# Output products for two pairs at a time, an output bias added by POOL, and a new order of slots in a gated attention and expert kernel

## What is computed

```python
def _L0_xattn_ref(Q, K, V, Wq, Wk, Wv, Wo):          # 16 heads, DK = DV = 64
    scores = einsum('bhqd,bhkd->bhqk', q, k) / sqrt(DK), causal mask
    out = einsum('bhqk,bhkd->bhqd', softmax(scores), v)
    return out.reshape(b, sq, H * DV) @ Wo

def _L0_ffn_ref(x, ...):
    h = _rmsnorm(x, gamma1)
    q = h @ Wq + bq;  k, v = split((h @ Wdown + bdown) @ Wup + bup)
    att = softmax(einsum('bthd,btgd->bthg', q, k) / sqrt(8))   # over the 16 heads of a row
    x = x + (einsum('bthg,btgd->bthd', att, v).reshape(b, t, D) @ Wo + bo)
    h2 = _rmsnorm(x, gamma2)
    gate = softmax(h2 @ Wg + bg)
    return x + einsum('btd,edf,bte->btf', h2, We, gate)

x = x + tanh(g_xattn[0]) * _L0_xattn_ref(_layernorm(x), ctx, ctx, Wq, Wk, Wv, Wo)
x = x + tanh(g_ffn[0]) * _L0_ffn_ref(_layernorm(x), ...)
```

## Time and profile before

| what | value |
|---|---|
| median of 3 runs | 261.29 us (259.64 to 261.53) |
| time of the profiled run | 261.93 us |
| its span | 259.9 us |
| PE busy | 245.6 us, 94% |
| DVE busy | 192.4 us, 74% |
| ACT busy | 171.6 us, 66% |
| POOL busy | 149.9 us, 58% |

### The profile page before, as it was taken

One profiled execution on the slowest core, in us unless ns is written; L12 is line 12 of the kernel. 1 busy time (PEld: TensorE's weight loads), 2 busy tenths in 40 slices (PEclk: granted clock), 3 DMA queues, 4 the chain that ended last, 5 costly groups with the idle time before them and its releaser, 6 DMA issues.

```text
span 259.9 us, 7887 instructions
## 1 busy us (share of the span) xinstructions
PE 245.6 (94%) x3244; PEld 178.7 (69%) x3244; DVE 192.4 (74%) x333; ACT 171.6 (66%) x501; POOL 149.9 (58%) x157
## 2 busy tenths in 40 slices
PE   7989989998899999999999999988999897979995
PEld 4765877785867677676859595858676462858774
DVE  0237644189998989898998842799989999786964
ACT  2437634756687787978787778566877676472454
POOL 4104041264646686969696835778466995867320
PEclk9999999999999999999999999999999998899999
DMA  6990000000000000000000000000000000000000
GB/s 208 359 320 21 3 4 3 3 1 3 3 3 0 3 10 3 15 0 15 1 3 13 3 11 3 13 3 10 3 0 5 11 14 3 11 0 3 10 13 20
DMA packets 6017, 7.30 MB, mean 28 GB/s; under 512 B 477, under 2 KB 4830, under 8 KB 5982
## 3 DMA queue, kind: packets, MB, share of 16 engines
q1 hardware_dynamic: 5550, 6.16, 7.5%
q10 hardware_dynamic: 432, 0.64, 0.7%
HBM read 5.88 MB, written 0.92 MB: 26 GB/s over the span
## 4 chain that ended last, share of the span: by engine, by line
PE 70%; DVE 18%; ACT 5%; issue 4%; POOL 1%; DVEq 0%; POOLq 0%
PE ps_a L875 40%; PE ps_c L875 9%; PE ps_b L875 8%; PE ps_e L875 7%; PE ps_b L927 4%; DVE ps_e L665 3%; DVE prod L683 3%; DVE ps_e L694 2%; ACT probs L446 2%; DVE nmax L626 2%; PE ps_b L872 1%; DVE psums L631 1%; DVE fqkv L649 1%; POOL prod L326 1%; PE ps_c L971 1%
## 5 line engine op out<-in xcount | busy, mean ns | idle before, releaser
L326 POOL TENSOR_TENSOR prod<-fqkv 128x1280 f32<-128x1280 f32 (+1 forms) x14 | 38.7, 2761 | 10.3 <-DVE fqkv L649 10.3
L316 POOL TENSOR_TENSOR probs<-probs,prinv 120x672 f32<-120x672 f32 x16 | 24.3, 1518 | 31.1 <-DVE prinv L635 31.1
L334 POOL TENSOR_TENSOR prod<-e_sb,fqkv 128x768 f32<-128x768 f32 (+1 forms) x14 | 24.5, 1753 | 21.3 <-ACT e_sb L474 21.3
L875 PEld LDWEIGHTS ps_a<-aT,wo_sb 128*128 128x128 f32 x256 | 30.8, 196 | 4.4 <-ACT v_sb L435 2.6
L875 PE MATMUL ps_a<-aT,wo_sb 128*128 128x112 f32 x256 | 32.1, 279 | 0.4 <-ACT aT L440 0.3
L875 PE MATMUL ps_a<-wv_sb,cT 128*64 128x512 f32 x128 | 32.3, 620 | 0.0
L665 DVE TENSOR_REDUCE ps_e<-prod 128x256 f32<-128x2048 f32 x13 | 29.7, 2287 | 0.0
L694 DVE TENSOR_REDUCE ps_e<-prod 128x128 f32<-128x2048 f32 x13 | 29.7, 2285 | 0.0
L875 PE MATMUL ps_a<-cT,wk_sb 128*128 128x224 f32 x128 | 28.6, 375 | 0.0
L429 ACT COPY kT<-ps_a 128x448 f32<-128x448 f32 x32 | 17.1, 533 | 16.2 <-PE ps_a L875 16.2
L875 PE MATMUL ps_a<-xT,wqc 128*128 128x224 f32 x128 | 27.1, 361 | 0.6 <-ACT qT L429 0.6
(11 more groups left out here) (144 smaller groups left out, 487.9 us busy)
## 6 DMA issues: line engine op xcount, KB each, us to landing
xp_sb<-in_xp SPq DMA_DIRECT2D x1, 896.0 KB, 7.9
out<-out_sb SPq DMA_DIRECT2D x14, 64.0 KB, 1.5
xT<-in_x_t SPq DMA_DIRECT2D x1, 784.0 KB, 9.5
cT<-in_ctx_t SPq DMA_DIRECT2D x1, 784.0 KB, 11.1
wv_sb<-in_wv SPq DMA_DIRECT2D x1, 512.0 KB, 8.1
wo_sb<-in_wo SPq DMA_DIRECT2D x1, 512.0 KB, 12.7
fwe_sb<-in_fwe SPq DMA_DIRECT2D x1, 512.0 KB, 8.8
fw_sb<-in_fw SPq DMA_DIRECT2D x1, 266.0 KB, 13.1
```

The lines of the kernel that those rows point to most:

```text
L316: nc.gpsimd.tensor_tensor(pr[0:TG, NC:C, :, 0:S], pr[0:TG, NC:C, :, 0:S], prinv[p % 2][0:TG, NC:C, :].unsqueeze(3).to_broadcast([TG, C - N ...
L326: nc.gpsimd.tensor_tensor(o, k, q, ALU.mult).then_inc(s["prod1_pool"], 1)
L334: nc.gpsimd.tensor_tensor(o, e, v, ALU.mult).then_inc(s["prod2_pool"], 1)
L875: return nc.tensor.matmul(o, lhsT, rhs, start=start, stop=stop, skip_group_check=True)
```

## The change

The first eight pairs are done two at a time in `new_y` and `new_x1`: one output product of 8 matmuls with 224 columns instead of two with 112 (`Y_UNITS`), in slots 2, 4, 6 and 8. Pair 0's product is no longer in the start. Since a tile may need both pairs of a unit, the slot that starts no tile is now slot 3, not slot 9 (`tile_steps`). `aT` is one tensor of two halves. `bias_o` is gone from PE; ACT scales `xc` in place (`scaled_x`), POOL adds the bias row (`biased`), and DVE's `new_x2` is a plain addition. The two warm-up products are seven of 128 columns. The order within the slots changes on all four engines.

```diff
+DOUBLE = 8
+Y_UNITS = [(p, p + 1) for p in range(0, DOUBLE, 2)] + [(p,) for p in range(DOUBLE, NP)]
+Y_AT = {unit[-1] + 1: n for n, unit in enumerate(Y_UNITS)}
+def units_for(f):
+    return next(n + 1 for n, unit in enumerate(Y_UNITS) if (unit[-1] + 1) * T >= (f + 1) * 128)
+def tile_steps():
+    steps, last = {}, 0
+    for f in range(NT):
+        last = max(last + 1, Y_UNITS[units_for(f) - 1][-1] + 1)
+        steps[last] = f
+    return steps
...
-        aT = two("aT", [128, C, T])
+        aT = sb("aT", [128, C, 2 * T])
...
+            def biased(f):
+                pool.wait_ge(s["u_ready"], f + 1)
...
+                nc.gpsimd.tensor_tensor(xc[f % XB][:, :], xc[f % XB][:, :], fw_sb[:, COL_BO:COL_BO + D], ALU.add).then_inc(s["ub_ready"], 1)
...
+            def scaled_x(f):
+                act.wait_ge(s["centred"], f + 1)
+                act.wait_ge(s["rstd2_ready"], f + 1)
+                nc.scalar.activation(xc[f % XB][:, :], xc[f % XB][:, :], ACT.Copy, scale=rstd2[f % XB][:, 0:1]).then_inc(s["u_ready"], 1)
...
-                nc.vector.scalar_tensor_tensor(out=x2[f % 2][:, 0:D], in0=xc[f % XB][:, :], scalar=rstd2[f % XB][:, 0:1], in1=ps_c[:, 1, 0:D],
-                                               op0=ALU.mult, op1=ALU.add).then_inc(s["x2_ready"], 1)
+                dve.wait_ge(s["ub_ready"], f + 1)
+                nc.vector.tensor_tensor(x2[f % 2][:, 0:D], ps_c[:, 1, 0:D], xc[f % XB][:, :], ALU.add).then_inc(s["x2_ready"], 1)
...
-            for n in (4, 3):
-                nc.tensor.matmul(ps_b[:, 0, 0:n * 128], ident[:, :], ident[:, :].unsqueeze(1).to_broadcast([128, n, 128]), start=True, stop=True)
+            for _ in range(7):
+                nc.tensor.matmul(ps_b[:, 0, 0:128], ident[:, :], ident[:, :], start=True, stop=True)
...
-                    ins = mm(ps_a[:, 0, 0:T], wo_sb[:, ch, :], aT[p % 2][:, ch, :], start=(ch == 0), stop=(ch == C - 1))
+                    ins = mm(ps_a[:, 0, 0:w], wo_sb[:, ch, :], aT[:, ch, c0:c0 + w], start=(ch == 0), stop=(ch == C - 1))
...
-                mm(ps_c[:, 1, 0:D], ident[:, :], fw_sb[:, COL_BO:COL_BO + D], stop=False)
```

More of the change, by code:

```diff
@@ L48, in sums_made @@
     return sum((by_pe.get(n, 0) > 0) + (by_pe.get(n, 0) < FH) for n in range(f + 1))
[L51 to L57, removed]
+DOUBLE = 8
[9 more added lines that the diff above has]
+    return steps
+TILE_AT = tile_steps()
+LAST_STEP = max(TILE_AT) + 2
 TAIL = 14
@@ L410, in _ @@
             second_scale(prior)
+            biased(last)
             gating(prior)
@@ L439, in attended @@
                 act.wait_ge(a_full[b], n)
-                nc.scalar.copy(aT[p % 2][:, 4 * half:4 * half + 4, :],
+                nc.scalar.copy(aT[:, 4 * half:4 * half + 4, p % 2 * T:(p % 2 + 1) * T],
                                ps_a[:, b, 0:4 * T].rearrange("p (c t) -> p c t", c=4)).then_inc(a_free[b], 1)
@@ L545, in _ @@
                     squares(fc)
+                if t < NP:
+                    exps(t)
+                if fc is not None:
                     x2_copy(fc)
@@ L550, in _ @@
                     head_exps(fb)
+                    scaled_x(fb)
+                if fc is not None:
+                    gate_exps(fc)
                 if t < NP:
@@ L603, in _ @@
             x2_copy(last)
+            experts(prior, 1)
             experts(prior, 0)
-            experts(prior, 1)
             gate_exps(last)
@@ L798, in _ @@
                     new_x2(fc)
+                if fb is not None:
+                    logits(fb)
+                if t in Y_AT:
+                    new_x1(Y_AT[t])
                 if t < NP:
                     prob_sums(t)
-                if t <= NP:
-                    new_x1(t - 1)
-                if t < NP:
                     norm(t)
                 if fb is not None:
-                    logits(fb)
                     shifted_logits(fb)
@@ L850, in _ @@
             shifted_logits(last)
+            gate_sum(third)
             head_scales(prior)
-            gate_sum(third)
             normed_heads(prior)
             weighted(last)
+            head_scales(last)
             new_x2(prior)
-            head_scales(last)
             head_sums(last)
@@ L859, in _ @@
             gate_logits(prior)
+            new_x2(last)
             gate_sum(prior)
-            new_x2(last)
             gate_logits(last)
@@ L1159, in _ @@
             turn_o(prior)
-            bias_o(prior)
             new_o(prior)
```

151 lines of the change are left out of this document (78 added, 73 removed).

## The result

The changed kernel takes 263.08 us (median of 11 executions, 262.4 to 264.8), the kernel before 260.95 (11, 259.5 to 261.8): a ratio of 1.0126, interval 1.0097 to 1.0155. The forecast was 258.1, faster. The profiled execution took 262.78 us with a span of 261.0.

The account below looks back on a forecast made before the run. PE was taken to set the pace, DVE 1.3 us behind in a full slot. Gains of 1.5 + 2.3 + 0.75, 4.5 us, less 1.3 for a lowered clock, gave 258.7, against the median 258.1 us; range 255.6 to 261.8.

Follow-up runs that it names:

- b_bias: The kernel before with only the output bias moved from PE (ACT scales the centred rows, POOL adds the bias), all orders kept: 262.16 us, 1.0078.
- b_warm: The kernel before with only its two warm-up products (512 and 384 columns) replaced by seven of 128 columns: 262.52 us, 1.0098.
- b_pad40: The kernel before with ten tiny products (40 more PE instructions) in PE's idle time ahead of the first scores: 262.71 us, 1.0085.
- a_pad36: The changed kernel with nine tiny products (36 more PE instructions) added: 267.65 us, 1.0276 against the kernel before.
- a_sums35: The changed kernel with DVE's probability sums and norm ahead of its logits in slots 3 and 5 only: 264.91 us, 1.0186 against the kernel before.
- b_pad112: The kernel before with 28 tiny products (112 more PE instructions) ahead of the first scores: 270.41 us, 1.0407.
- a_oldwarm: The changed kernel with the old two warm-up products (512 and 384 columns), 20 fewer records: 262.41 us, 1.0072 against the kernel before.

## What to carry over

Before taking a product's length off a busy engine, look at what the next instruction there waits for: two starts and the end of the copy between them show whether the product was cover. A product moved to another engine can delay a third: in b_bias POOL's bias addition moved its products onto DVE's scaling. Compare profiles with the granted clock of many executions in hand, since the one profiled may be unusual by more than the change. And where a loss appears in rows that the change didn't touch, count PE's instructions up to it: an edit of 20 instructions at the start of this kernel costs 2 us, by the profiles of b_warm and b_pad40 mostly in stops in the middle.

## What the hardware showed unexpectedly

Waiting for nothing that a row names, PE stopped for up to 3.69 us; 27 of 28 such stops lie where a count of 256 instructions ended inside or shortly behind the short products of `scores`, and each time PE went on 2.2 to 2.9 us after a 16 KB instruction packet began. A break between runs of equal products cost 0.07 to 0.13 us each, though PE's records show no gap. DVE's product of two SBUF tiles (120x224, 0.39 us) took up to 0.92 us when it came while POOL multiplied two SBUF tiles, and ended 0.25 us behind that. The granted clock went to its lower level (0.50, 1.2 of 2.4 GHz) behind gaps of 2.9 us in after and a_pad36 and of 2.5 us in a_sums35, and behind the stop of 3.69 us in b_pad112, and stayed at its upper one behind the gap of 1.4 us in a_oldwarm.
